# Expert attention: scores from rounded and remaining parts of queries and keys in fp32r, key halves exchanged by DMA, result written over the input

## What is computed

```python
ss = sigmoid(x @ Ws).reshape(b, t, 8, 5); sd = sigmoid(x @ Wd).reshape(b, t, 8, 5)
ms, md = topk_mask(ss, 3), topk_mask(sd, 3)          # 3 of 5 experts
q5 = (x @ Wq).reshape(b, t, 8, 5, 64)
k5, v5 = (x @ Wkv).reshape(b, t, 2, 8, 5, 64)[:, :, 0], [:, :, 1]
q = einsum('bthed,bthe->bhtd', q5, sd * md)          # the same for k and v with ss * ms
attn = softmax(einsum('bhid,bhjd->bhij', q * scale, k), axis=-1)
out = einsum('bhij,bhjd->bihd', attn, v)
o5 = einsum('bthd,dm->bthm', out, Wo).reshape(b, t, 8, 5, 128)
return einsum('bthem,bthe->btm', o5, md)
```

## Time and profile before

| | |
|---|---|
| median of 3 runs | 1888.64 us (1888.54 to 1892.25) |
| span of the profiled execution | 1890.9 us |
| TensorE busy | 1733.5 us (92%) |
| VectorE busy | 1139.3 us (60%) |
| ScalarE busy | 1271.8 us (67%) |
| GpSimd busy | 942.0 us (50%) |
| scores of the expert stage, L1174 | 1024 records, 261.7 us busy |

### The profile page before, as it was taken

How to read it: one execution, slowest core, us unless ns; L and a number is a source line. 1 busy time by engine, 2 the same in 40 slices (tenths; PEclk the granted TensorE clock), 3 DMA queues, 4 the chain that set the end, 5 groups by cost and what they waited for, 6 DMA issues and landing times. The chain is left out here.

```text
span 1890.9 us, 25427 instructions
## 1 busy us (share of the span) xinstructions
PE 1733.5 (92%) x8942; PEld 831.3 (44%) x8942; DVE 1139.3 (60%) x1868; ACT 1271.8 (67%) x2447; POOL 942.0 (50%) x566
## 2 busy tenths in 40 slices
PE   7888579999999999999999999889999999898975
PEld 3433255545555555555454554224333333332354
DVE  5887897986678876688766667332414123120296
ACT  2122115776777678676877777678898998999823
POOL 3555306788876788767888677840000000000033
PEclk9999699999999999999999999889999999999988
DMA  3000000000000000000000000130212212211001
GB/s 85 1 11 1 1 24 11 22 22 11 21 11 22 11 22 22 12 22 11 22 12 21 11 21 5 41 122 24 94 63 69 88 45 68 76 37 37 1 12 36
DMA packets 27863, 59.04 MB, mean 31 GB/s; under 512 B 3840, under 2 KB 14800, under 8 KB 27728
## 3 DMA queue, kind: packets, MB, share of 16 engines
q1 hardware_dynamic: 27728, 57.32, 9.5%
HBM read 38.44 MB, written 18.87 MB: 30 GB/s over the span
## 5 line engine op out<-in xcount | busy, mean ns | idle before, releaser
L894 POOL TENSOR_TENSOR b_psum<-b_psum,b_probs 128x1024 f32<-128x1024 f32 x192 | 463.8, 2416 | 154.2 <-ACT b_probs L1036 147.6
L2308 ACT ACTIVATE c_probs<-banks 128x1024 f32<-128x1024 f32 x512 | 483.5, 1030 | 47.9 <-PE banks L2357 36.8
L1381 DVE TENSOR_TENSOR b_gated<-banks,b_g 128x480 f32<-128x480 f32 x512 | 313.5, 654 | 199.8 <-PE banks L1141 187.7
L1036 ACT ACTIVATE b_probs<-banks 128x1024 f32<-128x1024 f32 x256 | 254.2, 1018 | 212.0 <-PE banks L1174 211.1
L1141 PE MATMUL banks<-b_w,b_xh 128*128 128x480 f32 x1024 | 351.8, 397 | 32.0 <-issue 14.3
L1389 DVE TENSOR_REDUCE b_tok<-b_gated 128x192 f32<-128x960 f32 x256 | 281.4, 1138 | 0.5
L1007 ACT ACTIVATE b_share<-b_o,b_picked 128x64 f32<-128x64 f32 x1080 | 268.7, 337 | 1.5 <-DVE b_o L1414 1.5
L1174 PE MATMUL banks<-b_qq,b_kk 64*128 64x512 f32 x1024 | 261.7, 623 | 1.1 <-DVE b_gated L1381 0.9
L2372 PE MATMUL banks<-c_probs,c_vg 128*32 128x512 f32 x2048 | 250.3, 606 | 2.9 <-DVEq L2423 2.6
L1206 PE MATMUL banks<-b_probs,b_tok 128*64 128x512 f32 x1024 | 249.2, 607 | 2.2 <-ACT b_probs L1036 2.2
L1141 PEld LDWEIGHTS banks<-b_w,b_xh 128*128 128x128 f32 x1024 | 193.6, 189 | 114.0 <-issue 45.9
(11 more groups left out here) (248 smaller groups left out, 1886.3 us busy)
## 6 DMA issues: line engine op xcount, KB each, us to landing
b_raw_w<-in_L_ffn_W SPq DMA_DIRECT2D x32, 480.0 KB, 3.3
c_heads<-c_split SPq DMA_DIRECT2D x24, 512.0 KB
c_keys<-c_heads SPq DMA_DIRECT2D x16, 512.0 KB, 3.7
c_queries<-c_heads SPq DMA_DIRECT2D x16, 512.0 KB, 4.7
c_heads<-c_split SPq DMA_DIRECT2D x8, 384.0 KB
a_xs<-in_L_attn_x SPq DMA_DIRECT2D x4, 512.0 KB, 8.2
out<-d_yo SPq DMA_DIRECT2D x3, 512.0 KB, 3.2
c_heads<-c_split SPq DMA_DIRECT2D x8, 128.0 KB
```

The lines of the kernel that those rows point to most:

```text
L894: nc.gpsimd.tensor_tensor(psum[:, par, :], prev, probs[:, i % 4, :], ALU.add).then_inc(psum_rdy, 1)
L1036: nc.scalar.activation(probs[:, i % 4, :], score_b[i % 2], ACT.Exp).then_inc(exp_rdy, 1)
L1381: nc.vector.tensor_tensor(shape(gated[:, t % 2, j, :]), shape(proj_b[u % WAYS][:, 0:HALF_W]), g.unsqueeze(2).broadcast_to([P, 3, HD2, E]), ...
L2308: nc.scalar.activation(probs[:, step % 4, c, :, :], unit_b[u % NU], ACT.Exp, scale=float(HD) ** -0.5).then_inc(exp_rdy, 1)
```

## The change

- `kk` and `qq` become fp32r and hold two parts. ScalarE writes the turned values rounded to fp32r (high part). VectorE subtracts that from the turned values in PSUM (low part): `low_keys` and `low_queries`, both in quarter 0, the first between the gate multiplications and the sums, the second behind the sums and ahead of the selection pieces.
- Each score step has three fp32r products for each half in place of one in fp32: high keys with high queries, low keys with high queries, high keys with low queries.
- The two copies of key halves into the other rows are gone from ScalarE. SyncE does this by two DMAs of 256 KB from SBUF to SBUF per head, which carry both parts, once `low_keys` is done.
- TensorE's waits on the copies become waits on `k_low`, `q_low` and, ahead of a head's first step, on the exchange.
- The result goes over the input: `r2` is gone, `out` is `x`. So that the redo path can start over, the input is first written to DRAM (`kept`, 2 MB), and the first norm waits for this.

```diff
-        kk = sb("kk", [P, 2, 2, HALF])
-        qq = sb("qq", [P, 2, HALF])
+        kk = sb("kk", [P, 2, 2, 2, HALF], F32R)
+        qq = sb("qq", [P, 2, 2, HALF], F32R)
...
+    SPLIT = ((0, 0), (1, 0), (0, 1))
+        out = x
...
         def _(sp):
+            if kept is not None:
+                sp.dma_start(kept[:, :, :], x[:, :, :]).then_inc(x_kept, 16)
...
+            def swap_keys(n):
+                sp.wait_ge(k_low, n + 1)
+                for at in (0, DH):
+                    other = DH - at
+                    sp.dma_start(kk[at:at + DH, n % 2, :, 1, :].bitcast(F32), kk[other:other + DH, n % 2, :, 0, :].bitcast(F32)).then_inc(swapped[n % 2], 16)
+
             def batch(b, first, last):
                 for h in range(NH):
                     if not (last and h + 3 >= NH):
                         front.load_weights(sp, b * NH + h + 3, (h + 3) % NH)
+                    if not (last and h == NH - 1):
+                        swap_keys(b * NH + h + 1)
+
+            swap_keys(0)
...
                 act.wait_ge(turn_ps, 2 * n + 1)
-                nc.scalar.copy(kk[:, par, 0, :], turn_b).then_inc(sides_rdy, 1)
-                nc.scalar.copy(kk[0:DH, par, 1, :], turn_b[DH:P, :]).then_inc(sides_rdy, 1)
-                nc.scalar.copy(kk[DH:P, par, 1, :], turn_b[0:DH, :]).then_inc(sides_rdy, 1)
+                nc.scalar.copy(kk[:, par, 0, 0, :], turn_b).then_inc(high_rdy, 1)
...
-                nc.scalar.copy(qq[:, par, :], turn_b).then_inc(sides_rdy, 1)
+                nc.scalar.copy(qq[:, par, 0, :], turn_b).then_inc(high_rdy, 1)
...
+                if kept is not None and b == 0:
+                    act.wait_ge(x_kept, 16)
...
             def turn_queries(n):
-                pe.wait_ge(sides_rdy, SIDES * n + 3)
+                pe.wait_ge(k_low, n + 1)
                 turn(n, 0)
...
                 if i == 0:
-                    pe.wait_ge(sides_rdy, SIDES * (n + 1))
+                    pe.wait_ge(q_low, n + 1)
+                    pe.wait_ge(swapped[par], 32 * (n // 2 + 1))
...
-                for side, (lo, hi) in enumerate(HALVES):
-                    rows = slice(DH * side, DH * side + DH)
-                    last = nc.tensor.matmul(score_b[i % 2][:, lo:hi], kk[rows, par, (side + i) % 2, i // 2 * P:(i // 2 + 1) * P], qq[rows, par, :], start=True, stop=not with_max)
+                for c, (k_part, q_part) in enumerate(SPLIT):
+                    for side, (lo, hi) in enumerate(HALVES):
+                        rows = slice(DH * side, DH * side + DH)
+                        last = nc.tensor.matmul(score_b[i % 2][:, lo:hi], kk[rows, par, k_part, (side + i) % 2, i // 2 * P:(i // 2 + 1) * P], qq[rows, par, q_part, :],
+                                                start=(c == 0), stop=(c == 2 and not with_max))
...
                         if has_next:
-                            pe.wait_ge(sides_rdy, SIDES * (n + 2))
+                            pe.wait_ge(q_low, n + 2)
                         turn_sums(n - 1)
...
+            def low_keys(n):
+                dve.wait_ge(high_rdy, 2 * n + 1)
+                nc.vector.tensor_tensor(kk[:, n % 2, 1, 0, :], turn_b, kk[:, n % 2, 0, 0, :].bitcast(F32), ALU.subtract).then_inc(k_low, 1)
+
+            def low_queries(n):
+                dve.wait_ge(high_rdy, 2 * n + 2)
+                nc.vector.tensor_tensor(qq[:, n % 2, 1, :], turn_b, qq[:, n % 2, 0, :].bitcast(F32), ALU.subtract).then_inc(q_low, 1)
...
+                    if p == 0 and has_next:
+                        low_keys(n + 1)
...
                         for t in steps:
                             sum_experts(n + 2, t)
+                    if p == 0 and has_next:
+                        low_queries(n + 1)
```

More of the change, by code:

```diff
@@ L715, in _, with switch_attention @@
                 pass
-def switch_attention(nc, x, out, ps, ident, I, place, signals, past, front, lead, recips, with_max, tag):
+def switch_attention(nc, x, kept, ps, ident, I, place, signals, past, front, lead, recips, with_max, tag):
     NH, E, DH, TOP = 8, 5, 64, 3
@@ L1186, in query_max @@
                     rows = slice(DH * (qt // 4), DH * (qt // 4) + DH)
-                    for part, (lo, hi) in enumerate(HALVES):
-                        last = nc.tensor.matmul(score_b[qt % 2][:, lo:hi], qq[rows, par, qt % 4 * P:(qt % 4 + 1) * P], kk[rows, par, part, :], start=True, stop=True)
+                    for side, (lo, hi) in enumerate(HALVES):
+                        for c, (k_part, q_part) in enumerate(SPLIT):
+                            last = nc.tensor.matmul(score_b[qt % 2][:, lo:hi], qq[rows, par, q_part, qt % 4 * P:(qt % 4 + 1) * P], kk[rows, par, k_part, side, :],
+                                                    start=(c == 0), stop=(c == 2))
                     last.then_inc(max_ps, 1)
@@ L1191, in query_max @@
                 if has_next:
-                    pe.wait_ge(sides_rdy, SIDES * (n + 1) + 3)
+                    pe.wait_ge(k_low, n + 2)
                 for half in range(2):
@@ L1517, in _ @@
                     sum_experts(n, t)
+            low_keys(0)
+            low_queries(0)
             run_periods(dve, period)
@@ L2859, in _, with redo_all @@
             last_norm(B - 1)
-def redo_all(nc, r1, r2, out_dram, ps, ident, I, pasts, flag):
+def redo_all(nc, r1, kept, out_dram, ps, ident, I, pasts, flag):
     signals = Signals(nc)
     sem = signals.names("redo_")
-    met, cleared = sem("met"), sem("cleared")
+    met, cleared, restored = sem("met"), sem("cleared"), sem("restored")
     for past in pasts:
@@ L2873, in redo_all @@
     with nc.sbuf_tensor("redo_recips", [P, RotaryLead.COUNTS], F32) as recips:
-        switch_attention(nc, r1, r2, ps, ident, I, nullcontext(expert), signals, None, None, None, recips, True, "b_redo_")
+        switch_attention(nc, r1, None, ps, ident, I, nullcontext(expert), signals, None, None, None, recips, True, "b_redo_")
     held = ExitStack()
@@ L2892, in _ @@
                 sp.wait_ge(cleared, 1)
+                sp.dma_start(r1[:, :, :], kept[:, :, :]).then_inc(restored, 16)
+                sp.wait_ge(restored, 16)
                 expert.sync_body(sp)
@@ L2906, in _ @@
                 pool.wait_ge(cleared, 1)
+                pool.wait_ge(restored, 16)
                 expert.gpsimd_body(pool)
@@ L2917, in _ @@
                 act.wait_ge(cleared, 1)
+                act.wait_ge(restored, 16)
                 expert.scalar_body(act)
@@ L2928, in _ @@
                 pe.wait_ge(cleared, 1)
+                pe.wait_ge(restored, 16)
                 expert.tensor_body(pe)
@@ L2939, in _ @@
                 dve.wait_ge(cleared, 1)
+                dve.wait_ge(restored, 16)
                 expert.vector_body(dve)
@@ L2968, in program @@
             expert, rotary, ending = Programs(), Programs(), Programs()
-            lead = RotaryLead(nc, middle, r2, ps, ident, I, "c_")
-            tail = switch_attention(nc, r1, r2, ps, ident, I, nullcontext(expert), middle, linear, front, lead, recips[:, 0:lead.COUNTS], False, "b_")
-            r3 = rotary_led(nc, r2, ps, ident, nullcontext(rotary), middle, lead, tail, lambda sp: weights.load(sp, I), recips, flag, "c_")
+            lead = RotaryLead(nc, middle, r1, ps, ident, I, "c_")
+            tail = switch_attention(nc, r1, kept, ps, ident, I, nullcontext(expert), middle, linear, front, lead, recips[:, 0:lead.COUNTS], False, "b_")
+            r3 = rotary_led(nc, r1, ps, ident, nullcontext(rotary), middle, lead, tail, lambda sp: weights.load(sp, I), recips, flag, "c_")
             weights = DepthWeights(lambda name, shape: lead.place("d_" + name, shape), depth.names("d_"))
```

16 lines of the change are left out of this document (8 added, 8 removed).

## The result

The changed kernel takes 1914.24 us (median of 4 runs, 1912.76 to 1918.51) against 1889.96 for the kernel before (4 runs, 1888.54 to 1892.25): a ratio of 1.0129, 95% interval 1.0111 to 1.0146. It is slower by 24 us, where I forecast 1890 and a range up to 1904.

A forecast was written before the change was run, and what follows sets the result against it. TensorE was taken to bound most periods of the expert stage and VectorE a few. Terms +3.2 - 0.45 + 5.2 - 6.1 - 7.2 + 7.4 - 0.1 - 1.0 = +0.95 us gave 1890 us, range 1878 to 1904.

The forecast's parts named there:

- pair pace of 0.23 us: Score products on TensorE: a pair of fp32r passes takes 0.23 us, bounds 0.21 and 0.33; two steps take 1.58 us.
- Plain periods: Nine expert-stage periods without selection work on VectorE or extra TensorE work: -0.68 us each, -6.1 together.
- Heads with TensorE work: Seven periods with transposes or output products on TensorE in quarters 2 and 3: 1.03 us won each, -7.2 together.
- The tail's -1.0: End of the expert stage: ScalarE drops two key copies in a row, -1 us, bounds 0 and -3.
- part 3: Eleven heavy heads, with selection work on VectorE: query subtraction delays pieces and gates, +5.2 and +7.4 us.
- rival D: VectorE stalls feed on each other, one and a half times part 3, plus clock falls, +3: 1899 us, chance 0.19.
- Rival B: VectorE's losses in the heavy heads are about half, +6.3 instead of +12.6 us: 1882 us, chance 0.23.
- E: All of the 44 us that the score products can win come through: 1846 us, chance 0.03.
- C: Weight loads of the score products are bare, 0.33 us a pair; gains vanish, losses stay: 1904 us, chance 0.10.
- part 1: Score products on TensorE: two steps take 0.34 us less, at most 44 us in the kernel.
- F: Score pairs don't run side by side in fp32r with 64 rows, two steps take 2.86 us: 2010 us, chance 0.03.
- The start: First head of the expert stage: key subtraction stands behind VectorE's warm-up work, first odd step 2.9 us late; +3.2 us in all.

The follow-up runs named there:

- experiment 6: Changed kernel with TensorE repeating the score products of step 2 in heads 2, 3 and 4 of the first three batches, scores unchanged: 1904.06 us.
- experiment 1: Changed kernel with the query subtraction behind the selection and norm pieces of quarter 0 instead of ahead of them: 1886.66 us, ratio 0.9962.

## Why the prediction was wrong

**Right, and shown.** The pair pace of 0.23 us, by the 1.59 us for two steps (1.58 forecast). Plain periods -0.76 each (-0.68 forecast), and the exchange, 3.6 us to land against 3.7 taken, with no engine waiting for it at the start, where the DMAs are issued at 278.50 and the first score goes at 284.86. The copy of the input landed in 6.5 us and held nobody. Heads with TensorE work won 0.86 each where 1.03 was forecast.

**Right by luck.** The tail's -1.0. The measured parts are +1.4 in head n = 30, -0.7 to the end of the stage and -1.8 in stages that the change doesn't touch; and head n = 30 moves with the falls of the clock, from +1.4 to -1.4 in experiment 6, where its code is the same.

**The step that failed is the size of part 3**, +12.6 forecast, bounds 6.3 to 18.9, +30.4 measured. The mechanism that it names is there: query subtraction ahead of the pieces, VectorE idle for ScalarE's copy (2.0 us at most in the waits of after, 1.95 forecast), gates late, odd steps behind them. Head 2 shows it nearly by itself, at +8.2 us. But part 3 priced the displaced pieces at their old durations and TensorE at its full clock, and both were wrong:
- *GpSimd's additions, 23.7 us.* Without those into the mixed result the heavy heads are at +6.7. I took the durations of the pieces from where they stood in the trace of before. At n = 11 two of them took 2.05 us there and 3.88 after. But in sum the pieces got only 2.9 us longer (99.1 to 102.0), so most of the cost isn't that they are longer, but where they are held up. That VectorE, with a wait and two subtractions more in quarter 0, has no idle time left to take the collisions up, so that they delay the gates, is my reading of the tables above, not shown by a run of its own. My bounds even counted on the opposite: the lower one supposed that displaced pieces would be shorter.
- *The clock, 7.8 us.* These aren't to be added: 7.5 of them lie in heads 3 and 4, where the clock doesn't fall at all once the additions are out, where TensorE's wait for the gates is shorter (1.23 us at n = 11 against 3.63). I had named the clock in rival D with 2 or 3 places at 3 us in all; it fell in ten. A clock of 0.5 inside the stage was also one of the signs of being wrong.

The 12.6 can't be split into a part without collisions and one with them, since the kernel before ran with them too.

**Rival D was right in kind and too small,** 1899 instead of 1914. It multiplied part 3 by one and a half; the factor is 2.4. Rival B (half the losses) and E are refuted, C too: bare loads would have shown a pair pace of 0.33. The rule of the Trainium skill about weight loads of the same row group, cited in part 1 ("TensorE: Matmul & The Clock Gate", Part 3), would have made 1.98 us for two steps; the trace has 1.59. F is refuted by the same row.

**The start** was mis-sized by about 1 us: +4.2 with the first head, +3.2 forecast. The first score itself is 5.8 us late within the stage, where about 3 were forecast. The wait for `low_keys` is in it as worked out, but the transposes and projections behind it ran at half the clock. Timeline of after:

```profile
277.79 0.68 DVE L1405 TENSOR_TENSOR b_kk<-banks,b_kk 128x512 fp32r<-128x512 f32 x1
...
278.52 1.11 PE L1172 MATMUL banks<-ident,b_tok 128*128 128x128 f32 x4 [4.97 <-DVE b_kk L1405]
...
284.86 1.66 PE L1190 MATMUL banks<-b_qq,b_kk 64*128 64x512 f32 x12
```

TensorE idles 4.97 us, then four transposes take 1.11 us where 0.66 is usual, and the first score starts 6.3 us after their start, where it was 3.6 before (273.11 to 276.75).

**Open:** the kernel before without GpSimd's additions was not run, so how much it loses to them itself is unknown; its copy of L285 at 1.03 us, against 0.32 alone, says that it is something. No run took out GpSimd's additions of probabilities, with which pieces collide as well, and none had the additions out and the repeated products in.

## What to carry to other kernels

When a change moves an elementwise operation on VectorE, look at what GpSimd does at the new place, not only at how long the operation took at the old one: here two pieces that need 1.46 us took 3.88. And ask what waits for it there: in experiment 1 the pieces took 105.2 us and the heavy heads lost 5.1, in the changed kernel 102.0 and they lost 30.4. An inserted wait belongs behind the work that doesn't need it; moving one subtraction behind a few pieces turned a loss of 24 us into a small gain. Where a change makes TensorE wait for some microseconds, count the slower products behind the wait as well.

## What was unexpected in the hardware

- A copy of 128x320 in fp32 on VectorE takes 0.32 us alone and 3.0 beside a 128x1280 addition on GpSimd; without these additions, 54 of them, the changed kernel is 26.5 us faster, although GpSimd is busy only half of the time.
- GpSimd is held up in turn: the addition of 2.95 us takes 3.41 when a VectorE piece starts ahead of it (run of experiment 1).
- Products that are repeated for nothing made the kernel 9.5 us faster. The heavy heads, where the granted clock stays at 1.00, are 7.8 us shorter, and a head in which nothing is repeated 2.8.
